# Masking transposed scores on VectorE, and splits and layer norm on GpSimd, in a latent attention block

## The reference

```
xn   = layernorm(x)
q    = xn Wq            16 heads of 64
lat  = xn Wkv_down      one latent of 64 per token
k, v = lat Wk_up, lat Wv_up
attn = softmax(causal(q k / sqrt(64)));  y = attn v;  a = y Wout
f    = tanh(xn weight aux1 aux2 + bias)
out  = x + a + f
```

## Time and profile before

| | us |
|---|---|
| median of 3 runs | 2001.67 |
| the three runs | 2001.54, 2001.67, 2013.03 |
| the profiled execution | 2006.04 |
| its span | 2004.3 |
| PE busy | 1966.3 (98%) |
| PE weight load | 1327.7 (66%) |
| DVE busy | 1360.3 (68%) |
| ACT busy | 1157.7 (58%) |
| POOL busy | 1482.9 (74%) |

### The profile page before, as it was taken

The page is one execution under the profiler, slowest core; times in us unless marked ns, Lnnn a source line. Parts: engine busy times, 40 slices in busy tenths (PEclk is TensorE's granted clock), DMA queues, the critical chain, the costliest instruction groups (busy, mean ns, idle before and its releaser), DMA issues.

```text
span 2004.3 us, 34226 instructions
## 1 busy us (share of the span) xinstructions
PE 1966.3 (98%) x11208; PEld 1327.7 (66%) x11208; DVE 1360.3 (68%) x3619; ACT 1157.7 (58%) x2203; POOL 1482.9 (74%) x1291
## 2 busy tenths in 40 slices
PE   8999999999999999998999999999999999999997
PEld 6766666676666676765666666666767666676754
DVE  5778665796667765687666876668756687565761
ACT  4565565565555565564565555655656556565653
POOL 0677677786777777875777877778768787777786
PEclk8999999999999999999999999999999999999998
DMA  4222122221222212221121221222221222121210
GB/s 125 54 61 59 37 73 57 65 62 44 54 57 72 72 43 50 62 78 41 44 62 50 79 59 36 59 57 75 60 54 49 55 75 57 52 54 54 52 44 30
DMA packets 117825, 116.48 MB, mean 58 GB/s; under 512 B 24208, under 2 KB 100880, under 8 KB 117648
## 3 DMA queue, kind: packets, MB, share of 16 engines
q1 hardware_dynamic: 117648, 114.29, 21.3%
HBM read 53.94 MB, written 8.91 MB: 31 GB/s over the span
## 4 chain that ended last, share of the span: by engine, by line
PE 91%; DVE 5%; ACT 2%; issue 1%; DMA 0%; POOL 0%; ACTq 0%; DVEq 0%; POOLq 0%; SPq 0%
PE ps L996 25%; PE ps L932 21%; PE ps L1010 14%; PE ps L980 13%; PE ps L983 12%; PE ps L1034 3%; DVE split_lo L1253 1%; DVE ps L1232 1%; PE ps L1023 1%; ACT probs L1140 1%; PE ps L1063 1%; ACT q_hi L1202 0%; DVE maxima L1237 0%; DVE acc L1281 0%; PE ps L809 0%
## 5 line engine op out<-in xcount | busy, mean ns | idle before, releaser
L1377 POOL TENSOR_TENSOR p_sum<-p_sum,probs 128x512 f32<-128x512 f32 x672 | 868.7, 1321 | 129.9 <-ACT probs L1140 127.7
L1140 ACT ACTIVATE probs<-ps 128x512 f32<-128x512 f32 x1152 | 667.7, 597 | 335.5 <-PE ps L983 320.6
L1232 DVE CUSTOM_DVE_ANT_0 ps<-ps,causal 128x512 f32<-128x512 f32 (+4 forms) x1024 | 521.0, 527 | 196.7 <-PE ps L1010 188.3
L996 PE MATMUL ps<-probs,latent 128*64 128x512 f32 x2304 | 518.1, 597 | 0.0
L980 PE MATMUL ps<-q_hi,k_hilo 128*128 128x512 f32 x1152 | 474.8, 412 | 6.9 <-ACT probs L1140 3.2
L1010 PE MATMUL ps<-k_hilo,q_hi 128*128 128x512 f32 (+4 forms) x1536 | 473.9, 356 | 2.8 <-DVE maxima L1232 1.2
L983 PE MATMUL ps<-q_lo,k_ones 65*128 65x512 f32 x1152 | 457.8, 397 | 0.0
L1377 POOL TENSOR_TENSOR p_sum<-probs 128x512 f32<-128x512 f32 x224 | 294.3, 1328 | 202.9 <-ACT probs L1140 202.2
L1237 DVE TENSOR_REDUCE maxima<-ps 128x1 f32<-128x512 f32 (+1 forms) x512 | 326.1, 637 | 147.3 <-PE ps L1010 143.6
L996 PEld LDWEIGHTS ps<-probs,latent 128*64 128x64 f32 x2304 | 156.2, 137 | 301.0 <-issue 297.6
L1010 PEld LDWEIGHTS ps<-k_hilo,q_hi 128*128 128x128 f32 x1536 | 282.6, 190 | 97.3 <-DVE maxima L1232 18.2
(11 more groups left out here) (102 smaller groups left out, 2261.4 us busy)
## 6 DMA issues: line engine op xcount, KB each, us to landing
q_hi<-q_hi SPq DMA_DIRECT2D x256, 128.0 KB, 2.4
norm<-recips SPq DMA_DIRECT2D x256, 128.0 KB, 2.9
q_lo<-q_lo SPq DMA_DIRECT2D x128, 128.0 KB, 2.3
x_in<-in_L_attn_x_bld SPq DMA_DIRECT2D x16, 512.0 KB, 4.5
acc<-in_L_attn_x_bld SPq DMA_DIRECT2D x32, 256.0 KB, 3.1
out_x<-acc SPq DMA_DIRECT2D x64, 128.0 KB, 1.7
q_lo<-rows SPq DMA_DIRECT2D x128, 4.0 KB
rows<-norm SPq DMA_DIRECT2D x128, 4.0 KB
```

Of the source, the lines that this page charges most:

```text
L996: last = nc.tensor.matmul(y_bank[g * LATENT:(g + 1) * LATENT, :], latent[par][:, key_block(unit, s), :], probs[:, t % PT_SLOTS, g * BANK:( ...
L1140: nc.scalar.activation(probs[:, t % PT_SLOTS, g * BANK:(g + 1) * BANK], ps[:, bank_of[kind, key], :], ACT.Exp).then_inc(exp_done, 1)
L1232: nc.vector.tensor_tensor_reduce(bank, bank, causal[:, BANK - w:BANK], 1.0, LOWEST, ALU.add, ALU.max, maxima[:, unit % 4, h, 0:1]).then_in ...
L1377: nc.gpsimd.tensor_tensor(sums, other, probs[:, slot, part], ALU.add).then_inc(pool_done, 1)
```

## The change

- The mask of a diagonal step is added to the scores in PSUM by DVE, between ST and exp, from a new table `future` (0 or -3.0e38). POOL's `affine_select` is gone; PV and R of a diagonal step wait for the exp instead of POOL, and the count that POOL's additions signal is numbered anew (`sums_added`).
- LO, LN4 and the last 12 steps of LN1 go from DVE to POOL. LN1 has 16 steps instead of 13, as POOL's Newton step takes four instructions where DVE's took three.
- F, tanh and FA work in the PSUM bank of F; `ff` is gone, and the bank is held until FA.
- PV uses four 32-column matmuls per step instead of two of 64.
- The tables and rules of `Order` change, and the start-up computes Q for the second half already, and places MT later.

The diff, cut (the waits that only renumber POOL's signal, and the constants of the start, are left out):

```diff
-LN1_PARTS = 13
+LN1_PARTS = 16
...
-            "F": (390, 520), "FA": (850, 950), "RC": (260, 340), "NM": (1140, 1200), "LO": (1140, 1200),
+            "F": (390, 520), "FA": (390, 520), "RC": (260, 340), "NM": (1140, 1200), "LO": (1140, 1200),
...
-LATER = {"O": 600, "R": 300, "MT": 300, "Q": 300}
-WIDTHS = {"PV": 64, "R": 32}
+LATER = {"O": 2000, "R": 300, "MT": 0, "Q": 300}
+WIDTHS = {"PV": 32, "R": 32}
...
-BATCH = 8
+BATCH = 6
...
-LEAD = 13
+LEAD = 14
...
             elif kind == "LN4":
-                self.xn[key] = self.run("DVE", when, DVE_TIME[kind])
+                self.xn[key] = self.run("POOL", when, (1400, 1500))
...
             elif kind == "LO":
-                self.normal[key] = self.run("DVE", when, DVE_TIME[kind])
+                self.normal[key] = self.run("POOL", when, (1300, 1350))
...
-        end = self.run("ACT", self.on_pe("ST", ready), ACT_TIME["ST"])
+        end = self.on_pe("ST", ready)
+        if s == 0:
+            end = self.run("DVE", end, (590, 680))
+        end = self.run("ACT", end, ACT_TIME["ST"])
...
-            idle_act = self.free["ACT"] < now + 300
+            idle_act = self.free["ACT"] < now - 300
             late = max(due, key=lambda c: step - c[1], default=None)
-            if late and (not st or step - late[1] > 0.5 or not idle_act):
+            if late and (not st or step - late[1] > 2.5 or not idle_act):
...
-    plan += [("W", "fold wvo"), *maxima[3:6], ("W", "fold wff"), *maxima[6:]]
-    plan += [("MT", 0), ("W", "split wvo")]
+    plan += [("W", "fold wvo"), *maxima[3:6], *two_parts("Q", (1, 0)), *maxima[6:]]
+    plan += [("W", "fold wff"), ("MT", 0), *two_parts("Q", (1, 1)), ("QL", (1, 0)), ("QD", (1, 0))]
+    plan += [("W", "split wvo"), ("QL", (1, 1)), ("QD", (1, 1))]
...
-                        if s == 0:
-                            wait_new(pool_done, 2 * t + g + 1)
-                        else:
-                            wait_new(exp_done, 2 * t + g + 1)
-                        last = nc.tensor.matmul(y_bank[g * LATENT:(g + 1) * LATENT, :],
-                                                latent[par][:, key_block(unit, s), :],
-                                                probs[:, t % PT_SLOTS, g * BANK:(g + 1) * BANK],
-                                                start=(s == 0), stop=(s == block_of(unit)))
+                        wait_new(exp_done, 2 * t + g + 1)
+                        for half in range(0, LATENT, WIDTH):
+                            row = g * LATENT + half
+                            last = nc.tensor.matmul(y_bank[row:row + WIDTH, :],
+                                                    latent[par][:, key_block(unit, s), half:half + WIDTH],
+                                                    probs[:, t % PT_SLOTS, g * BANK:(g + 1) * BANK],
+                                                    start=(s == 0), stop=(s == block_of(unit)))
...
-                    act.wait_ge(st_full, 2 * t + g + 1)
+                    if s == 0:
+                        act.wait_ge(st_masked, 2 * unit + g + 1)
+                    else:
+                        act.wait_ge(st_full, 2 * t + g + 1)
...
-                    nc.scalar.activation(ff[:, :], ff[:, :],
-                                         ACT.Tanh).then_inc(tanh_done, 1)
+                    f_bank = ps[:, bank_of["F", key], 0:D]
+                    nc.scalar.activation(f_bank, f_bank, ACT.Tanh).then_inc(tanh_done, 1)
...
-                if kind == "MAX":
+                if kind == "ST" and key[2] == 0:
+
+                    t, unit, s, g = key
+                    dve.wait_ge(st_full, 2 * t + g + 1)
+                    scores = ps[:, bank_of[kind, key], :].rearrange("p (h q) -> p h q", q=P)
+                    nc.vector.tensor_tensor(
+                        scores, scores, future.rearrange("p (a q) -> p a q", a=1).broadcast_to([P, 4, P]),
+                        ALU.add).then_inc(st_masked, 1)
+                elif kind == "MAX":
...
-                    nc.vector.tensor_tensor(ff[:, :], bias_all[:, :],
-                                            ps[:, bank_of[kind, key], 0:D],
+                    nc.vector.tensor_tensor(f_bank, bias_all[:, :], f_bank,
                                             ALU.add).then_inc(f_biased, 1)
...
+                elif kind == "LO":
+                    slot = key % SPLIT_SLOTS
+                    pool.wait_ge(norm_hi, key + 1)
+                    nc.gpsimd.tensor_tensor(split_lo[:, slot, :], y[:, key % Y_SLOTS, :],
+                                            split_hi[:, slot, :].bitcast(F32),
+                                            ALU.subtract).then_inc(norm_lo, 1)
...
+                elif kind == "LN4":
+                    b, k = key
+                    pool.wait_ge(ln_chain, chain_at(b, LN1_PARTS))
+                    for i in (2 * k, 2 * k + 1):
+                        last = nc.gpsimd.tensor_scalar(x_in[:, i, :], x_in[:, i, :],
+                                                       mean_var[:, i, 0:1], ln[:, 1, i:i + 1],
+                                                       ALU.subtract, ALU.mult)
+                    last.then_inc(xn_ready, 1)
...
-                if s == 0:
-
-                    v = probs[:, slot, part].rearrange("p (h q) -> p h q", q=P)
-                    nc.gpsimd.affine_select(
-                        out=v, in_=v, pattern=[[0, 4], [1, P]], compare_op=ALU.is_ge, fill=0.0,
-                        base=0, channel_multiplier=-1).then_inc(pool_done, 1)
-                    continue
```

126 lines of the change are left out of this document (65 added, 61 removed).

## The result

| | before | changed |
|---|---|---|
| median of the runs | 2003.7 us (1996.8 to 2037.0, 9 runs) | 2017.3 us (2014.4 to 2019.1, 9 runs) |
| ratio | | 1.0077, 95% interval 1.0058 to 1.0095 |
| profiled execution | 2006.0 us, span 2004.3 | 2017.3 us, span 2015.5 |

A forecast was written before the change was run, and what follows sets the result against it. PE, busy 98% of the span, was taken as the bound, so only its work and late starts counted. From the profiled 2006.0 us: -9.0 + 0 - 5.4 - 3.4 + 2.6 - 0.6 - 4.0 gave 1986 us, range 1966 to 2008.

The forecast's parts named there:

- gaps filled: Start: PE's waits of 1.36 us for the last maxima and 2.31 us for the row's DMA get filled, -3.4 us.
- norm: Start: 12 Newton steps on POOL instead of 9, plus 0.2 us for LN4, delay PE's first transposes, +2.6 us.
- clock: First 50 us: what the moved gaps do to PE's granted clock, taken as 0, between -3 and +3 us.
- LO: Split moved to POOL: the 6.64 us PE wait near 930 us, its slow clock and part of other waits go, -9.0 us.
- mask: Mask on DVE between ST and exp of diagonal tiles: mostly covered by PE's other work, 0 us (-3 to +41).
- columns: 32-column PV: no turn between PV and R, steps no slower, -5.4 us.
- small waits: PE's 110 weight-load waits for exps shrink without DVE instructions of uncertain length, -4 us (-11 to +5).
- end: Last LO slower on POOL, but earlier NM saves the last O its wait of about 1, -0.6 us (-2 to +2).
- no cost of four tiles: PV and R products: four tiles take 1.68 ns per column like two, 0 us; the per-matmul rival, chance 0.03, said 2044 us.
- The mask's own rival: Diagonal tiles: masks hold the two ST banks, 0.16 us exposed each, +41 us, 2027 us; chance 0.10.
- POOL late: Batch ends: LO and LN4 stand behind POOL's additions, transposes wait for LN4, 2004 us, no change; chance 0.12.

The follow-up runs named there:

- experiment 3: Changed kernel plus eight unused warm-up matmuls on PE right ahead of the first transposes: 2010.4 us, ratio 1.0021 to the kernel before.
- Experiment 1: Changed kernel with batch 0's last 12 reciprocal-square-root steps and LN4 back on VectorE, same order: 2008.0 us, ratio 1.0008 to the kernel before.
- experiment 10: Kernel of 8 with the start-up order of the kernel before (Q of the second half behind the first ST): 2002.8 us, ratio 0.9995.
- 15: Kernel before with only the 32-column values product and the feed-forward block in PSUM: 1987.8 us, ratio 0.9914.
- 16: Kernel of 15 with the split LO on GpSimd, mask left on GpSimd: 2009.3 us, ratio 1.0025 to the kernel before.
- 18: Kernel of 8 with the order rules of the kernel before: 2043.9 us, ratio 1.0188 to the kernel before.
- 17: Kernel of 15 with the changed kernel's rules for the order, six planner numbers: 2073.0 us, ratio 1.0343 to the kernel before.
- 14: Kernel of 13 with the mask back on GpSimd as well: 2077.4 us, ratio 1.0363 to the kernel before.
- 9: Kernel of 8 with the mask back on GpSimd as a select after the exp: 2016.6 us, ratio 1.0068 to the kernel before.
- 13: Kernel of 8 with the split LO back on VectorE for all 64 blocks, mask still on VectorE: 2058.0 us, ratio 1.0267 to the kernel before.
- 8: Changed kernel with batch 0's norm and the last four splits on VectorE: 2006.1 us, ratio 1.0008 to the kernel before.
- experiment 5: Kernel before with only the values product changed, four 32-column matmuls per step instead of two of 64, same order: 1992.9 us, ratio 0.9949.
- experiment 7: Changed kernel with each diagonal tile's mask added twice on VectorE, a third of the value each time: 2119.6 us, ratio 1.058 to the kernel before.
- experiment 4: Changed kernel with LO of the last four units on VectorE: 2015.3 us, ratio 1.0043 to the kernel before.

## Why the prediction was wrong

The sum had three parts that can be set beside the progress table (matched by work done the measured column is +14, -9 and +6).

| part | forecast | measured | error |
|---|---|---|---|
| start (gaps filled -3.4, norm +2.6, clock 0) | -0.8 | +12.7 | 13.5 |
| body (LO -9.0, mask 0, columns -5.4, small waits -4) | -18.4 | -8.9 | 9.5 |
| end | -0.6 | +7.3 | 7.9 |

**The start is the step that failed first and most.** Its term took LN4 on POOL as 0.2 us more, "about 0.4" an instruction, with an upper end of 0.6. Both had no row behind them: the nearest POOL rows were selects and two-input instructions, and the product at 512 columns, 1.30 us, would have given 0.65 for 256. The measured 1.21 is beyond even that. PE's first transposes need four LN4, and come 4.7 us later than before: 3.5 of it is LN4, where the term had 0.2, and 1.2 the Newton steps, where it had 2.4. And the clock, set to 0 within 3 us, is 4 to 7 us (experiment 3). Experiment 1 undoes the norm's part, 8 to 9 us; experiment 10 gives another 3 to 6 that the filled gaps were to save. Of the gaps of 3.67 us only 0.8 were saved, since 1.16 us for the row stayed and a new one of 1.68 for the maxima came.

**LO to POOL.** What the rows showed of the stall was right: it went, DVE has no instruction over 1.05 us, the clock is 1.00 in 900 to 1100, and matched by work done the changed kernel makes up 8.8 us there, where the term had 9.0. But this is a term of one place. As a statement on the move it was wrong. The experiments give the move in three surroundings, and one half of a fourth:

| rules for the order | mask on | split on VectorE | split on GpSimd |
|---|---|---|---|
| before | GpSimd | 1987.8 (15) | 2009.3 (16) |
| before | VectorE | not run | 2043.9 (18) |
| changed | GpSimd | 2073.0 (17), 2077.4 (14) | 2016.6 (9) |
| changed | VectorE | 2058.0 (13) | 2006.1 (8) |

The kernels of 8, 9, 13, 14 and 18 have the changed start and the later batches' norm on GpSimd; 15 to 17 have not, and 14 and 17 show that this matters by some 4 us. Under the old rules, with the mask on GpSimd, the split on GpSimd costs 21.5 us; under the new ones it gains 52 to 61. The ledger from before to after is then: columns and block in PSUM -17, split +21.5, mask, later norms and start +34.6, the rules -37.8, the norm and last splits of start and end +11.2, together +12.5, which is 2017.3 less the 2004.8 of the kernel before in those runs. Not one of my terms was the price of the rules, and on this path they are the largest item. It is one path through the runs, and another would share the sum out in another way: between 15 and 17 the same rules cost 85 us. I had read the rules' effect only in two stretches of the order. How the rules do it is shown for 17, where the splits meet POOL's rows, and not for 18.

**The columns** were right in mechanism. No turn between PV and R, 0.88 us a step, no cost of four tiles: eight records of 32 columns take what four of 64 took. Rule and row disagreed here, and the row was right: the overhead per matmul that the Trainium skill states (TensorEngine Tiling (Array Packing), Instruction Overhead) doesn't show in the mean of the 4608 records. In the order of before the term is 10.1 us (experiment 5), where the rows give 13.6. In the changed order, with 148 stretches, no run tried it. There -8.8 for the stall, -5.4 as forecast and +6.1 for the excess would make -8.1, and -8.9 was measured; the excess is not known to better than a few us, so this says only that nothing large is missing.

**The small waits** failed: forecast -4, measured +6.1. They were taken to follow from DVE's uncertain lengths, and these went, but the waits did not. Exps now wait for DVE's `ps<-ps,future` 181 us in all, but little of that reaches PE. Sorted by the tile whose exp they wait for, only 13 of the 125 waits of ST's weight loads stand behind a masked tile, 9.3 of the 38.4 us; before, 14 stood behind a diagonal tile, 4.6 of 36.2 us. So the mask adds about 5 us, and about 100 of the waits have no masked tile near them. The mask's own rival, 0.16 us exposed each, did not come: these 5 us are 0.02 each, and of a second mask 0.40 us shows (experiment 7).

**The end**: the last splits cost 2 us, as experiment 4 measured, where the term had -0.6; the R ahead of the last PV is argued from the rows, not shown.

**The rivals.** POOL late, 2004 us, stood for splits and LN4 behind additions. It named the right engine, but for the later batches, and PE's waits for POOL are four at the end (5.2 and 4.7 us in all) and one at the start. The rule that I set beside it, that VectorE is for two-input work and POOL takes about twice as long (the Trainium skill, GPSIMD Engine Reference, Engine selection), held for the split (1.28 against 0.69), while LN4, with one tensor input, is 3.7 times slower at the start (1.21 against 0.33). It was on the path once, and there it decided.

Left open are: how much of the excess belongs to the mask and how much to the later norms in experiment 18, the R at the end, and that kernels with the same start differ by up to 5 us in the first ST (54.1 in 13, 59.2 in 8).

## What to carry to other kernels

A stall that you remove is worth its length at its place; a move of work between engines is worth what the whole order makes of it, and the rules that set the order are a part of the change that needs its own price: here six numbers were worth 38 us one way and 85 the other. Price an operation on an engine that has never run it by the dearest neighbour, not the nearest, where PE has nothing else to do, and add the clock behind the wait. Of a change with several parts run the simplest one alone first: the 32 columns with the block in PSUM were 0.9% faster than before, and the whole was 0.8% slower.
